# Edge sums of a graph layer in pairs of groups, with eleven gather batches on TensorE in thirty groups

## What is computed

```python
msg = relu(x[src] + edge_attr @ We + be)
aggr = segment_sum(msg, dst, num_segments=6250)
h = (1.0 + eps) * x + aggr
h = relu(h @ W1 + b1) @ W2 + b2
h = (h - mean(h)) * rsqrt(var(h) + 1e-5) * gamma + beta   # over the nodes
out = layernorm(x + relu(h) + x)
```

## Time and profile before

| what | before |
|---|---|
| runs | 1677.64 us median of 3 (1674.07 to 1679.46) |
| span of the profiled execution | 1673.3 us; for this execution no other time is given |
| busy: PE, DVE, ACT, GpSimd | 94%, 74%, 44%, 72% |
| PE's granted clock, mean | 0.989 |
| DMA | 151.00 MB, mean 90 GB/s |

### The profile page before, as it was taken

One profiled execution on the slowest core, in us unless ns is written; L12 is line 12 of the kernel. 1 busy time (PEld: TensorE's weight loads), 2 busy tenths in 40 slices (PEclk: granted clock), 3 DMA queues, 4 the chain that ended last, 5 costly groups with the idle time before them and its releaser, 6 DMA issues. The chain is left out here.

```text
span 1673.3 us, 59216 instructions
## 1 busy us (share of the span) xinstructions
PE 1566.0 (94%) x21182; PEld 1221.0 (73%) x21182; DVE 1234.1 (74%) x3384; ACT 729.9 (44%) x1479; POOL 1207.5 (72%) x1244
## 2 busy tenths in 40 slices
PE   1289999999999999999999999999999999999984
PEld 1167777777777777777777777777777777777754
DVE  2787777777777777777777777777777777777555
ACT  0244444444444444444444444444444444444445
POOL 7377777777777777777777777777777777777732
PEclk9999999999999999999999999999999999999996
DMA  9633333333433333333333333333443333333422
GB/s 242 127 71 86 86 84 84 84 84 91 92 83 83 84 84 85 83 83 85 92 90 84 82 84 83 82 84 82 93 90 84 82 84 83 83 83 84 117 88 78
DMA packets 134449, 151.00 MB, mean 90 GB/s; under 512 B 45041, under 2 KB 114352, under 8 KB 134160
## 3 DMA queue, kind: packets, MB, share of 16 engines
q0 software_dynamic: 39360, 80.66, 19.4%
q1 hardware_dynamic: 87093, 60.01, 17.1%
q10 hardware_dynamic: 7963, 9.90, 2.1%
HBM read 144.07 MB, written 6.40 MB: 90 GB/s over the span
## 5 line engine op out<-in xcount | busy, mean ns | idle before, releaser
L507 POOL DMA_INDIRECT xg<-xb,idxb x1187 | 1150.9, 970 | 397.2 <-issue 326.6
L656 ACT ACTIVATE msg<-msg 128x512 f32<-128x512 f32 x390 | 245.5, 629 | 611.4 <-DVE msg L839 567.1
L1159 PE MATMUL ps<-hot,msg 128*128 128x64 f32 x3126 | 439.2, 284 | 34.6 <-ACT msg L656 18.9
L1159 PEld LDWEIGHTS ps<-hot,msg 128*128 128x128 f32 x3126 | 387.2, 194 | 88.1 <-ACT msg L656 22.7
L625 ACT ACTIVATE iota_all<-ps 128x384 bf16<-128x384 f32 x777 | 340.3, 488 | 178.6 <-PE ps L1221 173.3
L839 DVE TENSOR_TENSOR msg<-ps,xg 128x512 f32<-128x512 f32 x390 | 268.4, 688 | 91.3 <-PE ps L1154 87.4
L1240 PEld LDWEIGHTS ps<-iota_all 128*128 128x128 bf16 x4662 | 264.4, 98 | 70.6 <-issue 70.6
L1154 PE MATMUL ps<-we,ea 64*128 64x128 f32 x3126 | 285.5, 302 | 30.7 <-DVE msg L843 26.9
L1240 PE MATMUL ps<-iota_all 128*128 128x128 bf16 x4662 | 304.8, 219 | 0.0
L826 DVE TENSOR_TENSOR hot<-rel,iota 128x256 f32<-128x256 f32 x390 | 165.1, 423 | 176.0 <-PE ps L1159 127.9
L1154 PEld LDWEIGHTS ps<-we,ea 64*128 64x128 f32 x3126 | 209.4, 190 | 71.7 <-DVE msg L843 28.0
(11 more groups left out here) (134 smaller groups left out, 957.1 us busy)
## 6 DMA issues: line engine op xcount, KB each, us to landing
ea<-in_eat SPq DMA_DIRECT2D x156, 320.0 KB
xg<-xb,idxb POOLq DMA_INDIRECT x1187
accT<-in_xt ACTq DMA_DIRECT2D x1, 3125.0 KB
x<-in_xt ACTq DMA_DIRECT2D x1, 3125.0 KB
iota_all<-in_x ACTq DMA_DIRECT2D x1, 3080.0 KB, 38.7
out<-iota_all SPq DMA_DIRECT2D x5, 512.0 KB
xb<-iota_all SPq DMA_DIRECT2D x3, 784.0 KB, 5.8
idxb<-in_src_loop SPq DMA_DIRECT2D x78, 10.0 KB
```

Source lines behind the costliest of these rows:

```text
L507: pool.indirect_dma_start(out=xg[0:rows, slot, j, :], out_offset=None, in_=of, in_offset=bass.IndirectOffsetOnAxis(ap=index, axis=0)).then ...
L656: act.activation(msg[:, k, :, :], msg[:, k, :, :], ACT.Relu).then_inc(s_msg, 1)
L1159: last = pe.matmul(ps_win(), msg[0:r, k, j, :], hot[0:r, k, j, :], start=(m == 0), stop=(m == len(tiles) - 1))
```

## The change

- Groups go in pairs, 15 pairs a round, 13 rounds. On PE a pair is: linear of both groups in one visit, window of the pair before, pick, place, join, turn, pick, join, count.
- In `window` the one-hots (64 columns) are loaded and the 128 columns of messages run through; the first group's sums go to partitions 0 to 63, the second's to 64 to 127. ACT copies the result (`keep_sums`), PE transposes it (`turn`, line 1232), and DVE adds both halves.
- The lows go from PSUM through ACT to DRAM (`lowD`) and from there to all partitions (`lowB`) by two DMAs of SP. DVE compares in SBUF, f16, twice 128 x 896 (line 961). `share_lows` and the diagonal are gone.
- 11 batches in 30 groups instead of 9, each of seven steps (77 steps); three of them take two visits, the others three. `VISIT` says which steps fall in which half of a pair. Picks use three PSUM banks instead of two; `xg` has 15 slots instead of 10.
- The first 14 groups are gathered from x (and get the bias from DVE), not the first 10. Early chunks stand three to a pair in the last pairs but one. The doubling of xT is GpSimd's.

```diff
-    SORTED = (3, 6, 9)
-    SIZES = (3, 3, 3)
+    SORTED = (2, 5, 8, 10, 13, 16, 19, 21, 24, 27, 29)
+    FIRST = (-3, 0, 3, 6, 8, 11, 14, 17, 19, 22, 25)
+    SHARE = ((2, 3, 2), (3, 2, 2), (2, 3, 2), (4, 3), (3, 2, 2), (2, 3, 2), (3, 2, 2), (3, 4), (2, 3, 2), (3, 2, 2), (3, 4))
+    K0 = 5
+    K1 = 6
+    UNBIASED = 14
...
+            def spread_lows(j, k):
+
+                b = batch(j, k)
+                wait_apart(sp, s_low, b + 1)
+                if not isinstance(b, int) or b:
+                    wait_apart(sp, s_lowB, 16 * b)
+                sp.dma_start(lowD.rearrange("o (b r) -> (o b) r", r=CAP), lowS[:, :]).then_inc(s_lowD, 16)
+                if not isinstance(b, int) or b:
+                    wait_apart(sp, s_sel1, b)
+                wait_apart(sp, s_lowD, 16 * (b + 1))
+                sp.dma_start(lowB[:, :], lowD.partition_broadcast(P)).then_inc(s_lowB, 16)
...
+                    for j, k in phase(i, q, 2):
+                        ranks(j, k)
+                    add_x(i, 2 * q, n)
+                    for j, k in phase(i, q, 1):
+                        select_nodes(j, k)
+                    add_x(i, 2 * q + 1, n + 1)
+                    one_hot(i, q, pair)
...
+                        dve.wait_ge(s_turned, pair)
+                        for half in range(2):
+                            add_window(n - 2 + half, half, base_of[2 * (q % 5) + half - skip])
+                    for j, k in phase(i, q, 1):
+                        select_edges(j, k)
+                    for j, k in phase(i, q, 3):
+                        pairs_of(j, k)
...
+            def window(q, pair):
...
+                for j in range(GROUP):
+                    for half in range(2):
+                        last = pe.matmul(ps_win[half * WIN:(half + 1) * WIN, :], hot[:, q % TURN, half * GROUP + j, :],
+                                         msg[:, q % TURN, half * GROUP + j, :], start=(j == 0), stop=(j == GROUP - 1))
+                last.then_inc(s_win, 1)
...
+            def turn(pair):
+
+                pe.wait_ge(s_winS, pair + 1)
+                pe.transpose(ps_turned, winS[:, :], ident[:, :]).then_inc(s_turned, 1)
```

More of the change, by code:

```diff
@@ L340, in frame @@
[L340 to L357, removed]
-        def gathered(i, g):
[L361 to L366, removed]
@@ L368, in before, with at_step, phase, visit @@
-        def before(i, g):
+            return j * NB + k - K0
+        def at_step(j, k, t):
+            return batch(j, k) * NTILE + t
+        def phase(i, q, ahead):
+            found = []
+            for k in range(NB):
+                turn, step = divmod(FIRST[k] // 2 - ahead, STEPS)
+                if step == q:
+                    found.append((i - turn, k))
+            return [(j, k) for j, k in found if live(j, k)]
+        def visit(i, v):
+            if v < 0:
+                i, v = i - 1, v + VISITS
+            return [(i + turn, k, t) for turn, k, t in VISIT[v] if live(i + turn, k)]
@@ L434, in _ @@
             load_ea(0, 0)
[L435 removed]
+            for h in range(1, SPANS):
+                load_idx(0, h)
             load_ea(0, 1)
@@ new lines, in iteration @@
+                for q in range(STEPS):
+                    pair, n = i * STEPS + q, i * ROUND + 2 * q
+                    if closing(i, q) and q == CLOSE:
+                        act.wait_ge(s_st1, at_step(ITERS - 1, K1, NTILE - 1) + 1)
+                        act.dma_start(xT, xt).then_inc(s_xt, 16)
+                    for j, k in ending(i, 2 * (q - 1)):
+                        take(j, k)
+                    if not head or q:
+                        keep_sums(pair - 1)
+                    for j, k, t in visit(i, 2 * q):
+                        keep_rows(j, k, t)
+                    for j, k in phase(i, q, 2):
+                        keep_slots(j, k)
+                    for c in early(i, q):
@@ new lines, in iteration @@
+                for q in range(STEPS):
+                    pair, n = i * STEPS + q, i * ROUND + 2 * q
+                    for half in range(2):
+                        h, s = divmod(2 * q + half, SPAN)
+                        if s == 0:
+                            pe.wait_ge(s_ea[h % PARTS], (i * (SPANS // PARTS) + h // PARTS + 1) * 32)
+                        if half == 0 and (not head or q):
+                            pe.wait_ge(s_pre, n)
+                        linear(h % PARTS, s, half, ALL)
+                    if not head or q:
+                        window((q - 1) % STEPS, pair - 1)
+                    for j, k, t in visit(i, 2 * q):
+                        pick(j, k, t)
+                    for j, k in phase(i, q, 2):
+                        place(j, k)
+                    for j, k, t in visit(i, 2 * q - 1):
+                        join(j, k, t)
+                    if not head or q:
+                        turn(pair - 1)
+                    for c in early(i, q):
```

654 lines of the change are left out of this document (308 added, 346 removed).

## The result

The changed kernel takes **1901.41 us** (median of 4 runs, 1897.34 to 1904.0) beside 1675.97 of the kernel before: a ratio of 1.1326 on record, 95% interval 1.131 to 1.1343 (the two medians alone give 1.1345). Ratios here leave out executions that lie over 1.5% above a kernel's fastest. It is 13% slower where 1635 us was forecast. The profiled execution has a span of 1895.5 us; the forecast for the span was 1630, so 265.5 us have to be found.

What follows compares the result with a forecast made beforehand. PE was taken to bound the kernel, GpSimd within 1%. Start 120.6, 182 pairs at 117.1 us a round 1420.8, end 44.6 and 43.7 gave 1630, plus 4.3: 1635 us, range 1590 to 1690.

Steps and rivals of the forecast that it cites:

- PE's price list: Time of each PE step in a pair, from the timeline of before; 113.2 us a round for PE against 119.1.
- the halves of the columns run one behind the other: Rival on PE's sums: column halves not side by side, 13.5 us more a round, 1799 us; chance 0.05.
- side by side only in part: Rival on PE's sums: 0.25 us more for each visit, 3.8 a round, 1681 us; chance 0.04.
- Waits that it adds: Step on PE's counts waiting for DVE, 1.8 us a round, and the lows' trip through DRAM, 2.1.
- The counts' wait: PE's count at a pair's end waits for DVE's line 923; 2.6 us against 2.4 of cover, 1.8 a round.
- The lows' trip: Lows out to DRAM and back: 5.6 us plus 0.2 on ScalarE, 0.3 late; 2.1 us a round taken.
- a rival at 1690: Lows' two transfers take 8.5 us, not 5.8; DVE stands, PE waits 8.4 us a round; chance 0.13.
- the forecast 117.1: A round of 30 groups: PE's work 113.2 us plus waits 1.8 and 2.1, 1.7% under before.
- The end: Add of group 377 to that of 389 in 44.6 us; xT's doubling on GpSimd, which finishes gathers some 30 us early.
- The start: Fourteen groups from unshifted x, not ten; the fourteenth add done at 120.6 us, 12.6 us earlier.
- what lies behind the last add: Closing stretch after the last add: 43.7 us against 50.1, with xT's doubling moved and the last second product ahead.
- no wait costs anything: Rival: DVE starts early enough and the lows land in time, saving 3.9 us a round, 1588 us; chance 0.20.

Runs made afterwards that it cites:

- buffers: Against the changed kernel: three buffers in place of one for `slotS`, ScalarE's copy of the slots; 1754.05 us, 1.0479 of before.
- buffers, `pairs_of`: Against the changed kernel: three buffers for `slotS`, and VectorE's `pairs_of` moved ahead of its wait for the turned sums and the window adds; 1609.75 us, 0.9601 of before.
- the same, no loop: Against the kernel with three `slotS` buffers and `pairs_of` moved: the 13 rounds written out with no loop; 1570.95 us, 0.9361 of before.
- when `pairs_of` is out of the way: Against the changed kernel, one `slotS` buffer kept: only `pairs_of` moved ahead of the wait for the turned sums and the window adds; 1814.39 us, 1.0813 of before.
- the doubled trip: Against the kernel with three `slotS` buffers and `pairs_of` moved: one more DRAM-to-DRAM DMA in the lows' trip; 1782.06 us, 1.0623 of before.
- once GpSimd no longer held VectorE up: Against the changed kernel: doubling of xT taken from GpSimd, given to VectorE in two halves in the last round; 1891.18 us.
- without the other waits: Against the kernel with three `slotS` buffers, `pairs_of` moved and no loop: xT doubled by VectorE in place of GpSimd; 1558.38 us, 0.9287 of before.
- its body written out three times: Against the kernel before: its loop of 10 groups written out three times, body 30 groups; 1774.88 us, 1.0578 of before.
- two bodies: Against the kernel before: its loop written out twice, 17 turns; 1772.73 us median, 1.048 of before.

## Why the prediction was wrong

Rounds of 30 groups, from the windows of each kernel's adds and of its PE (busy and idle us of a round):

| kernel | round | PE busy | PE idle |
|---|---|---|---|
| before | 119.1 | 118.9 | 0.2 |
| changed | 139.5 | 120.0 | 19.5 |
| buffers | 125.9 | 116.1 | 9.8 |
| buffers, `pairs_of` | 116.2 | 112.9 | 3.3 |
| the same, no loop | 111.5 | 110.7 | 0.8 |

They come from these rows, of which the first is given above (for `changed`: 256 adds of line 909 in 1190 us, 1190 x 30 / 256 = 139.5; 1023.62 x 30 / 256 = 120.0). With buffers alone 262 adds stand in 1100 us with 1014.01 of PE's, with both edits 284 with 1068.51, without a loop 296 with 1091.84:

```profile
335.00:1435.00 1100.00, 1068.51 (x18389) 831.11 (x18390) 728.39 (x2487) 591.01 (x1475) 836.18 (x845) 0.99 0.46 110
```

- **PE's price list was right**, 2% too high. It said 113.2 us of work a round; the kernel without its waits and its loop shows 110.7 busy in a round of 111.5. One pair of the changed kernel, PE's timeline:

```profile
816.88 1.16 PE L1211 MATMUL ps<-we,ea 64*128 64x128 f32 x16
817.97 1.09 PE L1225 MATMUL ps<-msg,hot 128*64 128x128 f32 x16
818.99 1.16 PE L1271 MATMUL ps<-x,iota_all 112*32 112x384 bf16 x24
820.08 0.34 PE L1252 MATMUL ps<-identh,slot 128*128 128x128 f16 x3
...
820.53 1.18 PE L1286 MATMUL ps<-iota_all,hot_all 128*128 128x128 bf16 x18
821.54 0.28 PE L1232 MATMUL ps<-ident,winS 128*128 128x128 f32 x1
821.75 0.51 PE L1271 MATMUL ps<-x,iota_all 112*32 112x384 bf16 x8
```

  From start to start: linear 1.09 (forecast 1.09), sums 1.02 (1.06), three picks 1.09 (1.10), placing 0.45 (0.44), two joins 1.01 (1.11), turn 0.21 (0.25). The rivals by which the halves of the columns run one behind the other, or side by side only in part, both fell.
- **"Waits that it adds" is the step that failed.** It named two waits and took their sum as 3.9 us a round. It left out the third and largest: `keep_slots` waits for `select_edges` of the batch before. The code says so (`act.wait_ge(s_sel2, b)`), and I had written of ScalarE that it "gains the copy of the sums" and is under 80% busy, which answers the wrong question: a queue in order is late by what stands at its head, not by its load. In 7 of 11 places the two batches are one pair apart, so the copy falls into the same pair as the compares that free its buffer, and these come last in it. Removing it wins 147 us alone, and 205 (1814 to 1610) when `pairs_of` is out of the way.
- **The counts' wait** was rightly found, in its place and with its releaser, and mis-sized: 1.8 us a round were forecast by subtracting PE's 2.4 us of cover from VectorE's 2.6. It is worth 87 us alone, 144 (1754 to 1610) without the other wait. VectorE's side itself was longer: in the timeline above it starts 0.42 behind the turn (forecast 0.27), adds for 0.49 (0.43) and compares for 1.82 (1.61), 3.0 with `pairs_of`. That is 0.4 a pair and does not make 7.2 a round. The subtraction also took VectorE to be ready when the turn is done, and a pair to be evenly filled; that a late ScalarE makes it uneven and the waits feed each other is my reading, not shown by a run of its own.
- **The lows' trip**, 2.1 us a round in the sum and a rival at 1690: its price in the changed kernel is not seen in PE's waits, and where the two other waits are gone PE is idle for 0.8 us a round with the trip in place. Yet the doubled trip costs 172 us. The forecast that it lies at the edge was right.
- **The loop** was not in the prediction at all: 39 us by the runs, 3.9 a turn, and 4.7 a round within the rounds. In 335 to 1435 us of the run with both edits nine gaps before the linear make 27.0 us, 3.0 a turn, and behind each the trace's clock record has one stretch at 1.2 GHz, 30.7 us together, in all of which PE is busy; at half speed that costs 15.4 us, 1.7 a turn. Without the loop the record has a single such stretch. 3.0 and 1.7 make the 4.7.
- **The clock** neither. Of the 22.4 us by which a round of the changed kernel is longer than the forecast 117.1, PE's busy time holds 120.0 - 110.7 = 9.3 for the same records, at the granted clock of 0.93. The clock record agrees: of the changed kernel's 1190 us PE is busy for 145.6 us at 1.2 GHz, half of which is 72.8 us, 8.5 a round. It comes back as the gaps go (116.1, 112.9, 110.7), so I read it as a charge on the gaps of about half their length; no run here changed the clock by itself.
- **The end**: "the doubling of xT goes to GpSimd, which is done with its gathers" looked at GpSimd's time only. The stretch of the last adds took 57.3 against 44.6, and 47.5 once GpSimd no longer held VectorE up; without the other waits the edit is worth 12.6 us.
- **The start** and what lies behind the last add came out at 116.5 (120.6) and 42.2 (43.7).

The forecast of a faster kernel would have been right, and the rival "no wait costs anything" (1588) close, for the same change with three buffers, one line of VectorE moved and no loop: 1571. What stays open: what PE does in the gap of a turn (no view shows it), and why the kernel before has a second gap some 5 us behind the turn with its body written out three times, but only one gap with two bodies, as in the changed kernel.

## What to carry to other kernels

For each wait that a change puts on an engine, ask first what stands behind it in that engine's queue and who needs it; the engine's load says nothing on this. Where a copy overwrites the one buffer that another engine reads last in its turn, and both fall into the same period, give it another buffer before all else: here 1.5 KB a partition were worth 147 to 205 us. A period made longer to fit a pattern also makes the loop's body longer; look at the length of the branch on each engine once, and write the loop out if a turn costs.

## What the runs showed of the hardware

- PE's branch at a loop's turn: 0.21 us with 1,188 records of PE from branch to branch, 3.4 to 4.7 us with 2,373 and more. Behind it came one or two gaps and, at all but one of the turns, a stretch at 1.2 GHz: 5.1 us a turn with two bodies (81 us / 16), 9.6 with three (96 / 10), 3.9 in the new form (39 / 10).
- One GpSimd instruction of 16.07 us on SBUF held an operation of VectorE with two SBUF inputs for 15.69 us, in place of 0.68.
- Gaps of 3 us in PE's work were followed by 4 to 14 us at a granted clock of 0.50 to 0.63, in the windows shown above.
- Two halves of the columns of an fp32 product, with 64 columns of weights each, run side by side in full: 16 records of 128 columns in 1.02 us, as long as 16 in the two halves of the rows (1.09).
